# A transformer block on one core: a third PSUM bank set for the first gate and up products, late attention rows, a shorter Newton chain

## The reference

```python
x = _layernorm(x + _L0_attn_ref(x, wq, wk, wv, wo))
gate_out = x_flat @ (gate_t * gate_s[:, None]).T      # 2048 x 3584
up_out = x_flat @ (up_t * up_s[:, None]).T
hidden = jax.nn.silu(gate_out) * up_out
out = hidden @ (down_t * down_s[:, None]).T           # 2048 x 1024
return _layernorm(x + out)
```

## Time and profile before

| | us |
|---|---|
| median of 3 runs | 1888.71 |
| lowest and highest | 1885.76, 1890.27 |
| the profiled execution | 1892.16 |
| its span, first to last instruction | 1890.4 |
| mean granted TensorE clock of it | 0.987 of full |

### The profile page before, as it was taken

The page is one execution under the profiler, slowest core; times in us unless marked ns, Lnnn a source line. Parts: engine busy times, 40 slices in busy tenths (PEclk is TensorE's granted clock), DMA queues, the critical chain, the costliest instruction groups (busy, mean ns, idle before and its releaser), DMA issues.

```text
span 1890.4 us, 27531 instructions
## 1 busy us (share of the span) xinstructions
PE 1812.7 (96%) x10512; PEld 883.7 (47%) x10512; DVE 1187.1 (63%) x2047; ACT 709.2 (38%) x1112; POOL 557.5 (29%) x1039
## 2 busy tenths in 40 slices
PE   7889999999999988889999999999999999999997
PEld 4545655555555533334444444444444444444443
DVE  7877778668767763435544444655665665667645
ACT  5343444444434434335343343342232232222221
POOL 1354546456546555231000000211321111122114
PEclk9989999999999998999999999999999999999999
DMA  8543234334324297458554343549411121222301
GB/s 245 115 101 79 52 83 131 75 78 112 96 46 124 81 222 218 182 177 292 194 192 140 137 147 139 212 162 185 152 59 59 62 81 40 81 98 90 106 11 78
DMA packets 228164, 233.14 MB, mean 123 GB/s; under 512 B 183873, under 2 KB 184129, under 8 KB 228033
## 3 DMA queue, kind: packets, MB, share of 16 engines
q1 hardware_dynamic: 227168, 230.99, 41.2%
q10 hardware_dynamic: 864, 0.39, 0.1%
HBM read 122.55 MB, written 72.88 MB: 103 GB/s over the span
## 4 chain that ended last, share of the span: by engine, by line
PE 83%; DVE 7%; issue 3%; POOL 2%; SPq 2%; DMA 2%; ACT 1%; ACTq 0%; DVEq 0%; POOLq 0%
PE bank L1026 31%; PE bank L927 19%; PE bank L1047 13%; PE bank L1060 6%; PE bank L977 4%; PE bank L939 3%; PE bank L963 3%; PE bank L988 2%; SPq L1561 2%; DVE down_forms L1364 1%; PE bank L942 1%; DVE gate_blocks L1358 1%; POOL p_tiles L1424 1%; DVE row_max L1240 1%; DMA x_forms_spill<-x_parts 1%
## 5 line engine op out<-in xcount | busy, mean ns | idle before, releaser
L1026 PE MATMUL bank<-x_forms,weight_forms 128*128 128x512 f16 x3136 | 703.2, 380 | 23.1 <-DVE up_blocks L1348 7.7
L1026 PEld LDWEIGHTS bank<-x_forms,weight_forms 128*128 128x128 f16 x3136 | 305.5, 98 | 399.6 <-issue 20.1
L1112 ACT ACTIVATE p_tiles<-bank 128x512 f32<-128x512 f32 (+1 forms) x352 | 193.2, 557 | 295.6 <-PE bank L963 292.0
L1240 DVE TENSOR_REDUCE row_max<-bank 128x1 f32<-128x384 f32 (+3 forms) x352 | 219.5, 635 | 94.7 <-PE bank L942 93.9
L1047 PE MATMUL bank<-down_forms 128*128 128x512 f16 x1152 | 259.7, 381 | 2.4 <-issue 2.4
L927 PE MATMUL bank<-wq_parts,xT_parts 128*128 128x256 f16 x1536 | 217.3, 275 | 9.0 <-DVE wq_parts L1204 8.8
L1416 POOL TENSOR_SCALAR_AFFINE_SELECT p_tiles<-p_tiles 128x128 f32<-128x128 f32 (+2 forms) x352 | 138.6, 402 | 216.8 <-ACT p_tiles L1112 216.3
L1383 DVE TENSOR_TENSOR acc<-bank,acc 128x512 f32<-128x512 f32 x188 | 127.5, 686 | 109.2 <-PE bank L1060 57.8
L927 PE MATMUL bank<-wo_parts,att_parts 128*128 128x512 f16 x768 | 193.2, 384 | 2.5 <-DMA att_parts<-att_spill 2.5
L1047 PEld LDWEIGHTS bank<-down_forms 128*128 128x128 f16 x1152 | 113.0, 98 | 139.8 <-issue 5.1
L927 PEld LDWEIGHTS bank<-wq_parts,xT_parts 128*128 128x128 f16 x1536 | 144.2, 98 | 56.4 <-issue 13.9
(11 more groups left out here) (114 smaller groups left out, 1950.2 us busy)
## 6 DMA issues: line engine op xcount, KB each, us to landing
weight_forms_spill<-weight_forms SPq DMA_DIRECT2D x28, 896.0 KB, 7.4
weight_forms<-weight_forms_spill SPq DMA_DIRECT2D x28, 896.0 KB, 4.6
x_forms_spill<-x_parts SPq DMA_DIRECT2D x56, 256.0 KB, 2.6
w_page<-gateT SPq DMA_DIRECT2D x28, 512.0 KB, 4.8
w_page<-upT SPq DMA_DIRECT2D x28, 512.0 KB, 5.0
w_page<-downT SPq DMA_DIRECT2D x28, 512.0 KB, 5.4
att_spill<-att_made SPq DMA_DIRECT2D x64, 128.0 KB, 2.1
att_parts<-att_spill SPq DMA_DIRECT2D x16, 512.0 KB, 3.3
```

Of the source, the lines that this page charges most:

```text
L1026: t = nc.tensor.matmul(strassen[bank_set(use)][to][:, :], w_form[:, use % 4, A_FORMS[a_form], k * P:(k + 1) * P], xF[:, :, B_FORMS[b_form] ...
L1112: nc.scalar.activation(p32[j][:, h0:h0 + heads, :], bank[5 + m % 2][:, 0:heads * n].rearrange("p (h c) -> p h c", c=n), ACT.Exp, scale=SCO ...
L1240: nc.vector.tensor_reduce(mx[:, u % 2, i, h0:h0 + ROW_HEADS[i]], bank[3 + m % 2][:, 0:ROW_HEADS[i] * n].rearrange("p (h c) -> p h c", c=n) ...
```

## The change

Six edits.

- `bank_set`: uses 1 and 3 get a third set, banks 7, 3 and 2; uses 0, 2 and 4 have set 0 as before, and use 5 set 1. A use now depends on the use two before (`use_before`), use 1 on the last attention scaling, and use 5 on the last residual and on sum 1 of use 3. `PRODUCT_ORDER` swaps the last product of a use with the first of the next from use 0 on.
- The last head group has no `presum`; its `sums` multiply all four tiles by ones.
- `xF_load` of the first pass has a rank lower by one slot of 46.
- Tiles 13 and 15 (`att_late`) load their attention rows into a second buffer, `att_parts_late`. It lies where the third weight page and the k stack were, so these loads wait for `scores_over`. A tile's load waits for the projection of the last tile that had the same buffer (`att_before`).
- Two weight page buffers instead of three; a load waits for the cast two pages back.
- Newton steps written with two-scalar instructions, in 8 instructions: r is kept times -2, 16 and -8192, and the factor is taken out at the end. The planner's cost of it goes from 3.1 to 2.0.

The diff, cut to what the prediction speaks of:

```diff
 def bank_set(use):
...
-    return use % 2 if use > 3 else 0
+    return 2 if use in (1, 3) else use % 2
...
 PRODUCT_ORDER = [(use, i) for use in range(USES) for i in range(NPR)]
-for use in range(4, USES - 1):
+for use in range(USES - 1):
     if use != 2 * NF - 1:
         at = PRODUCT_ORDER.index((use, NPR - 1))
         PRODUCT_ORDER[at:at + 2] = reversed(PRODUCT_ORDER[at:at + 2])
...
+FORM_RANK = 1.4
...
+        final = q == NU * UG - 1
+        if j in (1, 2) and not final:
             put(PO, at + 4, .2 + REP * (S - (j + 1) * P) / 410, "presum", u, G, j,
                 after=[("pv", u, G, j)] + [("presum", u, G, 2)] * (j == 1))
         if j:
             continue
-        put(PE, at + 3.5, 1.5, "sums", u, G, takes="T", after=[("causal", *one), ("presum", u, G, 1)])
+        put(PE, at + 3.5, 3.0 if final else 1.5, "sums", u, G, takes="T", after=[("causal", *one)] + [("presum", u, G, 1)] * (not final))
...
+def att_late(tile):
+
+    return tile in (TILES - 3, TILES - 1)
+
+
+def att_before(tile):
+
+    earlier = [t for t in range(tile) if att_late(t) == att_late(tile)]
+    return earlier[-1] if earlier else None
...
     put(SY, end - 14, .4, "att_load", tile, moves=PAGE_MOVES, after=[("att_store", UNITS * (tile // NT + 1) - 1, G) for G in range(UG)] + (
-        [("proj", "out", tile - 1, 1, KD - 1)] if tile else []))
+        [("score_k", NU - 1, *KEY_USES[-1])] if att_late(tile) else []) + (
+        [("proj", "out", att_before(tile), 1, KD - 1)] if att_before(tile) is not None else []))
...
-    put(PO, end + 1, 3.1, "newton", row, after=[("norm_stats", row)])
+    put(PO, end + 1, 2.0, "newton", row, after=[("norm_stats", row)])
...
 def use_before(use):
-    return (use - 1 if use < 5 else None if use == 5 else use - 2) if use else None
+    return use - 2 if use > 1 and use != 5 else None
...
+            elif use == 5:
+                after += [("sum", 1, 1, 1)] if i == 2 else [("residual", TILES - 1, 1)]
+            elif use == 1:
+                after += [("att_scale", NU - 1, UG - 1)]
+            if i > 2:
                 after.append((("sum", n, w, 0), ("copy", n, w, 1), ("copy", n, w, 2), ("sum", n, w, 2))[i - 3])
...
-        put(SY, at - 6, .4, "w_load", w, r, c, moves=PAGE_MOVES, after=scores + ([("w_cast", *pages[i - 3])] if i > 2 else []))
+        put(SY, at - 6, .4, "w_load", w, r, c, moves=PAGE_MOVES, after=scores + ([("w_cast", *pages[i - 2])] if i > 1 else []))
...
-        at = SLOT * (NU - 1) + 1.4 * m if p == 0 else use_at[2 * NF - 1] + (i + 1) * one
+        at = SLOT * (NU - 2) + FORM_RANK * m if p == 0 else use_at[2 * NF - 1] + (i + 1) * one
...
-        strassen = [{"P": bank[4], "Y": bank[5], "Z": bank[6]}, {"P": bank[0], "Y": bank[1], "Z": bank[2]}]
+        strassen = [{"P": bank[4], "Y": bank[5], "Z": bank[6]}, {"P": bank[0], "Y": bank[1], "Z": bank[2]},
+                    {"P": bank[7], "Y": bank[3], "Z": bank[2]}]
...
-        w_page = [sb(BB, f"w_page{i}", [D], F32) for i in range(3)]
+        w_page = [sb(BB, f"w_page{i}", [D], F32) for i in range(2)]
+        att = [att, sb(BB, "att_parts_late", [2, KD, P], F16)]
...
-                            on.wait_ge(s_att_in, 16 * (w + 1))
+                            late = att_late(w)
+                            on.wait_ge(s_att_in[late], 16 * len([t for t in range(w + 1) if att_late(t) == late]))
                         on.wait_ge(s_lo, split_n["wo", 0, k] + 1)
                         dst, cols = bank[n % 2][:, :], slice(part * HALF, (part + 1) * HALF)
-                        left, right = att, wo_p
+                        left, right = att[att_late(w)], wo_p
...
-                    on.wait_ge(s_pre, 2 * (u * UG + G + 1))
                     trans_free((kind, *which))
-                    for j in range(2):
+                    tiles = 2
+                    if u * UG + G == NU * UG - 1:
+                        tiles = NT
+                    else:
+                        on.wait_ge(s_pre, 2 * (u * UG + G + 1))
+                    for j in range(tiles):
                         for h in range(REP):
                             t = nc.tensor.matmul(bank[TRANS][h * HD:(h + 1) * HD, j * P:S], ones[:, :], p32[j][:, h, :],
-                                                 start=j == 0, stop=j == 1, tile_position=(0, h * HD))
+                                                 start=j == 0, stop=j == tiles - 1, tile_position=(0, h * HD))
...
-                    if use == 5:
-                        on.wait_ge(s_proj_taken, len(taken))
+                    if use == 1:
                         on.wait_ge(s_mcopy, NU)
                         on.wait_ge(s_scale_att, 4 * NU * UG)
+                    elif use == 5:
+                        on.wait_ge(s_proj_taken, len(taken))
+                        on.wait_ge(s_blk, 3 * 3 + 2)
...
-                    on.wait_ge(s_newton, 14 * (n + 1))
+                    on.wait_ge(s_newton, 8 * (n + 1))
...
-                    on.wait_ge(s_wpage[n % 3], 16 * (n // 3 + 1))
+                    on.wait_ge(s_wpage[n % 2], 16 * (n // 2 + 1))
...
-                    for m in range(3):
-                        nc.gpsimd.tensor_tensor(w, r, r, ALU.mult).then_inc(s_newton, 1)
-                        on.wait_ge(s_newton, 14 * n + 4 * m + 1)
-                        nc.gpsimd.tensor_tensor(w, w, v, ALU.mult).then_inc(s_newton, 1)
-                        on.wait_ge(s_newton, 14 * n + 4 * m + 2)
-                        nc.gpsimd.tensor_scalar(w, w, -0.5, 1.5, ALU.mult, ALU.add).then_inc(s_newton, 1)
-                        on.wait_ge(s_newton, 14 * n + 4 * m + 3)
-                        nc.gpsimd.tensor_tensor(r, r, w, ALU.mult).then_inc(s_newton, 1)
-                        on.wait_ge(s_newton, 14 * n + 4 * m + 4)
-                    nc.gpsimd.tensor_tensor(w, mv[:, n % 2, 0:1], r, ALU.mult).then_inc(s_newton, 1)
-                    on.wait_ge(s_newton, 14 * n + 13)
-                    nc.gpsimd.tensor_scalar(w, w, -1.0, None, ALU.mult).then_inc(s_newton, 1)
+
+                    for m, times in enumerate((1.0, -2.0, 16.0)):
+                        nc.gpsimd.tensor_scalar(w, r, r, v, ALU.mult, ALU.mult).then_inc(s_newton, 1)
+                        on.wait_ge(s_newton, 8 * n + 2 * m + 1)
+                        nc.gpsimd.tensor_scalar(r, w, 3.0 * times ** 2, r, ALU.subtract, ALU.mult).then_inc(s_newton, 1)
+                        on.wait_ge(s_newton, 8 * n + 2 * m + 2)
+                    nc.gpsimd.tensor_scalar(w, mv[:, n % 2, 0:1], r, 1.0 / 8192.0, ALU.mult, ALU.mult).then_inc(s_newton, 1)
+                    on.wait_ge(s_newton, 8 * n + 7)
+                    nc.gpsimd.tensor_scalar(r, r, -1.0 / 8192.0, None, ALU.mult).then_inc(s_newton, 1)
...
-                    if tile:
-                        on.wait_ge(s_proj, proj_n["out", tile - 1, 1] + 1)
-                    e.dma_start(att[:, :, :, :].rearrange("p a k c -> p (a k c)"),
-                                att_dram[b, t].rearrange("p a k c -> p (a k c)")).then_inc(s_att_in, 16)
+                    if att_before(tile) is not None:
+                        on.wait_ge(s_proj, proj_n["out", att_before(tile), 1] + 1)
+                    if att_late(tile):
+                        scores_over(on)
+                    e.dma_start(att[att_late(tile)][:, :, :, :].rearrange("p a k c -> p (a k c)"),
+                                att_dram[b, t].rearrange("p a k c -> p (a k c)")).then_inc(s_att_in[att_late(tile)], 16)
...
                     n, (w, r, c) = w_n[which], which
-                    on.wait_ge(s_cast, n - 2)
+                    on.wait_ge(s_cast, n - 1)
                     scores_over(on)
                     ch = 2 * r % FC + c
-                    e.dma_start(w_page[n % 3][:, :].bitcast(I32), (gateT, upT, downT)[w][ch]).then_inc(s_wpage[n % 3], 16)
```

11 lines of the change are left out of this document (5 added, 6 removed).

## The result

The changed kernel takes 1869.8 us (median of 4 runs, 1867.74 to 1872.53) against 1889.0 for the kernel before in the same session: a ratio of 0.9902, 95% interval 0.9882 to 0.9922. It is 19.2 us faster, give or take some 4; the forecast was 14.8 faster, within the range, with the rival that more arrives (20.6) nearer: 1.4 us off against 4.4. The profiled execution took 1868.12 us, span 1866.4, mean granted clock 0.993 (before: 1892.16, 0.987). This pair lies 24.0 us apart, 5 more than the medians, so what is read off the pair has some us too many.

A forecast was written before the change was run, and what follows sets the result against it. TensorE bounds the kernel, busy 1812.7 of 1890.4 us, so only idle time can close. 9.0 + 1.8 + 1.7 + 1.6 + 1.7 - 1.0 = 14.8 us gives 1873.9 at the median, range 1866 to 1883.

The forecast's parts named there:

- more arrives: Rival, chance 0.20: cast wait filled, norm and copy give 3.3, clock holds near 710 us; 20.6 us gained, 1868.1.
- Banks: After attention, TensorE's waits on block sums, `hidden` and `silu` all close through the new bank set: 9.0 us.
- Late rows: In the passage to the feed-forward part, TensorE's wait for tile 15's attention row load goes: 1.7 us.
- The freed queue: SyncE's queue no longer held by tile 13's load: priced at nothing, bounds a loss of 3 and a gain of 1.
- Last head group: Behind the last scores, masks end sooner without the GpSimd pre-sum, TensorE sums more: 1.8 us, bounds 0 and 2.6.
- The weight cast: The first product also needs its first weight page's cast, so at most 2.6 us can be won there.
- Newton in the tail: At the kernel's end, six fewer GpSimd instructions at 0.27 us a step save 1.6 us.
- Newton in the passage: Use 3's copy behind tile 15's norm comes sooner and lost clock returns: half of 3.3 taken, 1.7 us, bounds 0 and 4.7.
- Two pages: Use 3's second weight page is loaded late with two buffers instead of three: 1.0 us lost, bounds 0 and 4.
- x1 forms sooner: Lower rank of first-pass form loads on SyncE's queue, before the row-maximum rows: 0, bounds 3 us both ways.
- The cast wait: TensorE's 2.2 us wait for weight casts after the last projection stays.
- What would show it: Signs: named waits gone, first product near 742.8, last Newton 2.2 us, last projection over near 831; wrong if passage idles over 20 us.

The follow-up runs named there:

- b_newt: The kernel before with the new 8-instruction Newton step alone, every queue in its old order: 1885.4 us, ratio 0.9974.
- n_same: The changed kernel with the old 14 Newton instructions but planner cost 2.0, so every order stays: 1874.5 us, ratio 0.9919.
- u_late3: The changed kernel with one attention row buffer for all tiles and three weight page buffers: 1881.4 us, ratio 0.9962.
- b_plan: The kernel before with only the planner's cost of a Newton step changed from 3.1 to 2.0, orders sorted anew: 1890.4 us, ratio 1.0007.
- q_two: The changed kernel with two more x1 form loads put ahead of the last row-maximum rows on SyncE's queue: 1868.9 us, ratio 0.9887.
- u_late: The changed kernel with one attention row buffer for all tiles, two weight pages kept: 1878.7 us, ratio 0.9944.

## Why the prediction was right, and where not

*The sum.* For the stage from the last q projection to the 28th product the steps were 9.0 + 1.8 + 1.7 + 1.7 - 1.0 = 13.2, for the tail 1.6. Read off the pair: 18.5, of which 14.3 are idle time, and 0.7. The bottleneck, the places and the sign were right. What was closed is what the earlier trace rows listed.

*Banks, 9.0.* Right in size as far as can be told (6.8 measured, 4.6 of uncertainty; 10.0 in the profile), and in kind: the four groups of waits fell from 12.0 with all of L1348's rows and L1175, L1358 in them to 1.4. But the step took them for the banks' own. They need the late rows: without these the load waits take the gain.

*Late rows, 1.7.* The term that was most mis-sized: 7.9. It failed at "TensorE for the load, 1.7 us", a wait measured in the old order and priced as if the order stayed. It grew to 7.6 us and a slower clock once no products lay between the tiles. The freed queue at nothing: SyncE's queue never held tile 13 back in the changed kernel, whose tiles ran without a gap. Banks and rows together were forecast at 10.7 and measured at 8.9: the sum held by luck, because the one edit's missing part was the other's.

*Last head group, 1.8.* Some 1.1 in its stage: 1.7 us less waiting for the forecast 2.3, 0.65 us more of sums for the forecast 1.0, which was worked out from 2.35 us, a row at a lower clock (0.60 over that stretch). The weight cast did not bind: it ended at 734.55 in the changed kernel, 1.1 us ahead of the first product.

*Newton in the tail, 1.6.* Wrong: 0.7. "Six fewer save 1.6 us" took the step of 0.27 for the new form as well. The same paragraph had the case in hand (0.1 us more for each of seven, 0.7 lost again, leaving 0.9) and dropped it.

*Newton in the passage, 1.7.* The mechanism named, norm to copy of use 3, is what b_newt shows in the old order, with 0.7 us; all waits there give 1.3. In the new order that wait is 1.1 with either chain, so its fall from 3.04 is not Newton's, and n_same idles only 0.2 us more. The term's other half, the lost clock, is not shown: it went from one place to another. With the tail, 2.0 us of idle time in the old order stand against the forecast 3.3; the times, 4.9 (2.8 to 6.8) and 3.2, would allow 3.3, but no stage shows it.

*Two pages, -1.0.* Nothing that can be told: a third page brings no gain in u_late3. The price of nothing, with the sum 15.8, was the better one. It goes with the Trainium skill (Trainium Kernel Development and Optimization, Best Practices), which asks for double buffers to overlap DMA with compute.

*x1 forms sooner, 0.* The rank did nothing, as said. The wait for the row-maximum rows did go in the profile, from 3.58 to 0.62, through the planned cost of Newton, which I had not followed into the queue. The pair gives 3.7 us for that stage, 1.6 of idle time (7.6 and 6.0) and 2.1 of busy time. But b_plan closes the wait and gains nothing, and q_two reopens 1.2 us of it and loses nothing. So the 3.7 can't be booked to it. The prediction had inferred that such an order would not matter from the Trainium skill (DMA: Bandwidth & Descriptors, Issuing engines are not separate DMA queues), by which starting a DMA usually takes little beside the DMA itself, and set 1.27 us of queue per load against it. A load does hold the queue that long and the wait does move, but the time of the kernel goes with the inference.

*The cast wait, 2.2.* It stayed, to the hundredth. That it was a matter of page order, and worth closing, the prediction did not see.

*More arrives.* Of the three parts of this rival the casts' wait did not close. The wait behind norm and copy fell by 1.9 us and its lost 1.7 were not lost, more than its 3.3, though not by Newton. In the stage around 710 us, "q to score", 2.1 us of busy time went, for its 2.0 from the clock, in this pair. That it came nearer is in part luck: clock moves between executions.

*What would show it.* The waits named are gone, no attention row is waited for, TensorE idles 11.0 us in the passage (windows above) for under 20, the row-maximum wait is 0.6, no cast is waited for behind 886. Wrong: the last Newton takes 3.07 us, not 2.2; the first product begins at 735.7, not 742.8, and the last projection is over at 822.2, not 831. Of the 7.1 us at the first product 2.5 were there before the stage and 3.7 come from "q to score".

*What stays open.* Banks and rows 8.9, Newton 3 to 5, pre-sums 1.1 make 13 to 15 of 19.2. The other 4 to 6 us are of the size of the uncertainty. A part may be the clock, higher in every execution of the changed kernel than in any of the kernel before; no run separates it from the waits.

## What to carry to other kernels

A wait measured in one order prices an edit only in that order: where a planner or list scheduler rebuilds the order, look at what will stand next to the waiting piece, and undo edits in pairs before crediting one of them. Count a dependent chain by the start-to-start step of the very instruction form, since fewer but fatter instructions may save half of what their number says. Where a cast waits behind a blocked one, change the order of the requests before adding a buffer: here it was worth more than the buffer. Split a stage's gain into idle time and busy time before booking it: the second moves with the clock, and one trace can't credit it to an edit.

## What was not expected of the hardware

On GpSimd, one element per partition, a tensor-scalar with two scalar operands from memory (L1458) has a mean of 363 ns, one with a constant and a scalar from memory (L1460) 370, and the next instruction starts 0.40 to 0.44 us behind its start in the last Newton; a tensor-tensor of the same size takes 190 to 278 ns on average, a tensor-scalar with two constants 195 ns, at a step of 0.27:

```profile
L1460 POOL TENSOR_SCALAR rstd<-rstd 128x1 f32<-128x1 f32 x96 | 35.5, 370 | 9.7
L1458 POOL TENSOR_SCALAR rstd<-rstd 128x1 f32<-128x1 f32 x96 | 34.8, 363 | 220.2 <-DVE rstd L1329 213.8
```

And the length of a wait did not decide alone whether TensorE's clock fell to its lower level behind it. Behind 2.59 us the next 24 matmuls took 5.34 us in the kernel before and 7.03 in b_newt. Behind 3.34 us the next 48 took 10.52 in u_late, behind 3.44 in u_late3 11.86. A part of the changed kernel's gain is of this kind, 4.1 of the 18.5 us in the stage, time of TensorE's busy side that no list of waits shows.
